# States of two batches summed on TensorE, keys of the first batch made ahead of x, a threshold by a sign on ScalarE, and an order of its own for each engine

## The reference

```python
def step(state, xs):                      # L0: 16 states per channel, 256 channels
    d_t, B_t, C_t, u_t = xs
    dA = jnp.exp(d_t[..., None] * A)
    state = state * dA + (d_t * u_t)[..., None] * B_t[:, None, :]
    return (state, jnp.einsum('ben,bn->be', state, C_t))
y = y + D[None, :, None] * u              # y: the sum over the 16 states
y = y * jax.nn.silu(z)                    # z = layernorm(x)
...
q = rmsnorm(x_n @ Wq, gq)                 # L2: 16 heads of 128
k = rmsnorm(ctx @ Wk, gk)                 # needs the context alone, not x
...
scale = jnp.mean(jnp.abs(w)) + EPS        # L1 ffn, L2 ffn: six weights of 256 x 1024
q = jnp.clip(jnp.round(w / scale), -1.0, 1.0) * scale
...
x = x + tanh(g_xattn[0]) * L0_ssm(ctx, ln(x));  x = x + tanh(g_ffn[0]) * L0_moe(ln(x))
x = x + tanh(g_xattn[1]) * L1_smoothquant(ln(x), fside, ctx);  x = x + tanh(g_ffn[1]) * L1_ternary(ln(x))
x = x + tanh(g_xattn[2]) * L2_attention(ln(x), ctx);  x = x + tanh(g_ffn[2]) * L2_bitlinear(ln(x))
x = x + tanh(g_xattn[3]) * L3_attention(ln(x), ctx);  x = x + tanh(g_ffn[3]) * L3_ternary(ln(x))
```

## Time and profile before

| | us |
|---|---|
| median of 3 runs | 1147.06 |
| lowest, highest | 1143.35, 1147.12 |
| the profiled execution | 1148.34 |
| its span | 1146.6 |
| busy: PE, DVE, ACT, POOL | 837.9, 760.7, 523.6, 322.3 |
| mean granted clock of PE | 0.852 |

### The profile page before, as it was taken

The page is one execution under the profiler, slowest core; times in us unless marked ns, Lnnn a source line. Parts: engine busy times, 40 slices in busy tenths (PEclk is TensorE's granted clock), DMA queues, the critical chain, the costliest instruction groups (busy, mean ns, idle before and its releaser), DMA issues.

```text
span 1146.6 us, 12868 instructions
## 1 busy us (share of the span) xinstructions
PE 837.9 (73%) x3924; PEld 624.4 (54%) x3924; DVE 760.7 (66%) x1812; ACT 523.6 (46%) x1244; POOL 322.3 (28%) x394
## 2 busy tenths in 40 slices
PE   3111676646998977589799885898998769899455
PEld 2000355325666855357578664576886646667234
DVE  5898789874366787955688989554558654355542
ACT  5544543213554544455554553465344435556223
POOL 1433054403132103513444115224110331500204
PEclk9555589759999999789799998898999879989657
DMA  6511524424222202212323104124320221400002
GB/s 219 184 55 51 188 96 147 157 68 146 69 98 97 69 19 69 69 49 90 120 79 108 54 28 120 42 83 142 100 68 28 74 83 42 133 25 23 1 0 65
DMA packets 45476, 96.24 MB, mean 84 GB/s; under 512 B 4824, under 2 KB 16480, under 8 KB 44256
## 3 DMA queue, kind: packets, MB, share of 16 engines
q1 hardware_dynamic: 36192, 70.26, 19.0%
q0 software_dynamic: 9216, 25.17, 7.6%
HBM read 85.97 MB, written 9.44 MB: 83 GB/s over the span
## 4 chain that ended last, share of the span: by engine, by line
PE 45%; DVE 31%; issue 10%; ACT 9%; POOL 5%; DVEq 0%; POOLq 0%; ACTq 0%
PE bk L994 33%; PE bk L1045 7%; DVE ssm_u L1557 6%; DVE ssm_u L1563 2%; DVE ssm_u L1551 2%; PE bk L1240 2%; PE bk L1038 1%; DVE mx L1775 1%; DVE lnbuf L1465 1%; DVE t1A L1586 1%; DVE arB L1788 1%; PE bk L1376 1%; ACT arB L885 1%; DVE t2A L1589 1%; DVE t1B L1871 1%
## 5 line engine op out<-in xcount | busy, mean ns | idle before, releaser
L585 POOL TENSOR_TENSOR sy<-sy,ssm_u 128x512 f32<-128x512 f32 x64 | 86.6, 1354 | 110.6 <-DVE ssm_u L1563 104.2
L994 PE MATMUL bk<-hTA,ringT 128*128 128x256 f32 x448 | 116.6, 407 | 1.1 <-ACT hTB L769 0.7
L994 PE MATMUL bk<-bc,sel 96*128 96x512 bf16 x64 | 29.4, 463 | 97.3 <-DVE ssm_u L1563 93.6
L994 PEld LDWEIGHTS bk<-hTA,ringT 128*128 128x128 f32 x448 | 90.6, 207 | 17.5 <-issue 2.0
L557 POOL TENSOR_TENSOR lnbuf<-lnbuf,mhalf 128x2 f32<-128x2 f32 x32 | 23.4, 730 | 263.9 <-DVE lnbuf L1471 263.9
L1557 DVE TENSOR_TENSOR_SCAN ssm_u<-ssm_da,ssm_u 128x512 f32<-128x512 f32 x64 | 91.1, 1424 | 4.3 <-DVE ssm_u L1551 0.5
L994 PE MATMUL bk<-qk 128*128 128x256 f32 x288 | 80.4, 404 | 6.0 <-ACT arB L885 3.2
L885 ACT ACTIVATE arB<-bk,nb,rqs 128x256 f32<-128x256 f32 x128 | 71.0, 562 | 27.6 <-DVE nb L1778 27.4
L994 PE MATMUL bk<-arB,cx 128*128 128x256 f32 x256 | 69.5, 394 | 11.8 <-DVE qk L1823 8.9
L600 POOL TENSOR_TENSOR arA<-t2A,arA 128x256 f32<-128x256 f32 x44 | 38.0, 865 | 130.2 <-DVE t2A L1589 113.9
L803 ACT ACTIVATE ssm_da<-sdl,nega 128x255 f32<-128x255 f32 x128 | 57.1, 499 | 34.0 <-DVE ssm_u L1557 30.8
(11 more groups left out here) (326 smaller groups left out, 2249.4 us busy)
## 6 DMA issues: line engine op xcount, KB each, us to landing
ringT<-in_w SPq DMA_DIRECT2D x56, 384.0 KB, 3.0
ring<-q3s POOLq DMA_DIRECT2D x32, 384.0 KB, 3.3
ringQ<-in_wqk SPq DMA_DIRECT2D x32, 384.0 KB, 2.9
ring<-q7s POOLq DMA_DIRECT2D x32, 384.0 KB, 3.3
ringM<-m4s SPq DMA_DIRECT2D x32, 256.0 KB, 2.6
q3s<-qk SPq DMA_DIRECT2D x4, 512.0 KB, 7.7
q7s<-qk SPq DMA_DIRECT2D x4, 512.0 KB, 4.3
qk<-in_wo SPq DMA_DIRECT2D x4, 512.0 KB, 4.6
```

The costliest lines, as they stand in the source:

```text
L585: g.tensor_tensor(sy[:, :, :], sy[:, :, :], two(ssm_u[:, n % 3, :]), ALU.add).then_inc(*sig("s0.pool", "y", n))
L994: return t_.matmul(dst, lhsT, rhs, start=start, stop=stop)
```

## The change

1. **States on PE for batches 0 and 1.** `YB = {0: W1, 1: PT}` names a bank for each. In these batches POOL adds nothing; PE adds sy and then the product of each state into the bank, by fp32 products with the identity, 128x512: 17 per batch, 34 in all. The gate multiply reads the bank. Batches 2 and 3 stay on POOL.
2. **Keys of batch 0 ahead.** A new part `keys0` makes the 16 keys of batch 0 and adds their squares into the right half of the norm bank AR, in the banks SC and OP, once `value_output` is done. s4(0) then makes the queries only: its squares and its norm products are 256 wide, and no key is copied. The query and key weights are read eight slots (384 KB each) more often.
3. **Lower threshold by a sign.** ACT computes Sign(w + t), 128x2048, six times; DVE takes the minimum of (w > t) and the sign. The six marks on DVE and one of the two threshold instructions are gone.
4. **Banks and loads.** The group means of `group_ternary` and the products of `value_output` use the two banks SC and OP (four and two before). `weights2`, the refills and copies of the preparation have places of their own; x and the context of batch 1 are loaded first of all; the first reduction of `weights2` stands in the prologue.
5. **Order.** `PLAN` has one table for each engine, chosen by `now[0]`, with more points.

The core of the diff follows; its pieces stand in the order of the file: tables, SP, POOL, ACT, PE, DVE.

```diff
-        wthr, e0 = cut(lnbuf, e0, 2, 6)
+        wthr, e0 = cut(lnbuf, e0, 6)
...
-        GMB, M4B = [SC, PT, OP, SC], [SC, PT]
+        YB = {0: W1, 1: PT}
+        GMB, M4B, KB = [SC, OP], [SC, OP], [SC, OP]
...
+        now = [None]
         PLAN = {
...
-            "state": [((-1.2, 24.56), (2.23, 42.06), (5.66,...
...
+            "pe": {
...
+                "state": {0: ((-1.2, 155.15), (-0.2, 204.66...
...
-            knots = PLAN[part][b]
+            knots = PLAN[now[0]][part][b]
...
+            def fillK():
+                for j in range(NH // 2):
+                    yield at_kp(max(j - 1, 0) - 4)
+                    if j >= NQ:
+                        sp.wait_ge(*at(None, "k0.pe", "k", j - NQ))
+                    sp.dma_start(slotQ(j), a["wqk"][j]).then_inc(dma_sem(f"ringQ{j % NQ}"), 16)
...
+                if b in YB:
+                    return
                 for n in range(NST):
...
+                    yield at_ternary(n + 0.5)
+                    act.wait_ge(*at(None, "prep.dve", "thr", n))
+                    s.activation(q7b[n % 2], stage_slot[n % 2], ACT.Sign, bias=wthr[:, n:n + 1]).then_inc(*sig(K, "sgn3", n))
...
+            def keys0():
+                for j in range(NH // 2):
+                    yield at_kp(j + 0.4)
+                    act.wait_ge(*at(None, "k0.pe", "k", j))
...
+                    s.activation(N4[0][0][:, j % 2, :], KB[j % 2][:, :], ACT.Square).then_inc(*sig("k0.act", "sq", j))
+                    s.activation(kT[:, 2 * j:2 * j + 2, :], halves(KB[j % 2]), ACT.Copy, scale=gqk[:, 2:3]).then_inc(*sig("k0.act", "kT", j))
...
+            def keys0():
+                for j in range(NH // 2 + 1):
+                    if j < NH // 2:
+                        yield at_kp(j)
...
+                        for h in range(2):
+                            i = mm(half(KB[j % 2], h), slotQ(j)[:, (3 * h + 2) * P:(3 * h + 3) * P], cxTs[0][:, :])
...
+                            i = t_.matmul(B4[0][5][0:96, S:], hot[:, 15 - n:111 - n], N4[0][0][:, (j - 1) % 2, h * S:h * S + S],
+                                          start=n == 0, stop=n == NH - 1, skip_group_check=True)
...
+                def add_y(n):
+                    if n == 0:
+                        pe.wait_ge(*at(b, "s0.pool", "yd", 1))
+                        mm(YB[b][:, :], ident[:, :], sy[:, :, :].rearrange("p e t -> p (e t)"), stop=False)
+                    pe.wait_ge(*at(b, "s0.dve", "hc", n))
+                    mm(YB[b][:, :], ident[:, :], ssm_u[:, n % 3, :], start=False, stop=n == NST - 1).then_inc(*sig("sy.pe", "y", n))
...
+                if b == 0:
+                    pe.wait_ge(*at(None, "k0.act", "kT", NH // 2 - 1))
+                    pe.wait_ge(*at(1, "sx.dve", "yg"))
                 transpose_h(b, "s4", h, bank)
...
-                        mm(ring[n % 2][:, S:], w[:, 2 * P:], cxTs[b % 3][:, :]).then_inc(*sig("s4.pe", "kq", n))
+                        if b:
+                            i = mm(ring[n % 2][:, S:], w[:, 2 * P:], cxTs[b % 3][:, :])
...
-                    v.tensor_scalar(wthr[:, 1, n:n + 1], wmean[:, n:n + 1], -0.5, None, ALU.mult).then_inc(*sig(K, "thr", n))
-                    v.tensor_scalar(q7b[n % 2], stage_slot[n % 2], wthr[:, 1, n:n + 1], None, ALU.is_lt).then_inc(*sig(K, "lt", n))
-                                           in1=q7b[n % 2], op0=ALU.is_gt, op1=ALU.subtract).then_inc(*sig(K, "used", n))
+                    dve.wait_ge(*at(None, "prep.act", "sgn3", n))
+                                           in1=q7b[n % 2], op0=ALU.is_gt, op1=ALU.min).then_inc(*sig(K, "used", n))
```

241 lines of the change are left out of this document (157 added, 84 removed), and 210 rows, old and new, of the table PLAN.

## The result

| | before | after |
|---|---|---|
| median of the runs | 1145.55 us (1143.35 to 1147.12) | 1080.59 us (1077.70 to 1082.69, 4 runs) |
| ratio, 95% interval | | 0.942 [0.9393, 0.9447] |
| profiled execution: own time, span | 1148.3, 1146.6 us | 1082.7, 1080.9 us |

The change makes the kernel 65 us faster (the kernel before ran once more beside it, so its median is of four here). Most executions of the kernel before lie near 1144 or near 1149 us, and the profiled one is of the second kind, so a difference of 3 to 5 us between two single traces can be one between executions.

The account below looks back on a forecast made before the run. No one engine bounds the whole: DVE bounds the states, short dependent chains some stretches, PE from 281 to 1001. Terms -8 - 3 + 3 + 2 - 14 - 12 = -32 gave 1116.3, about 1115 by median; range 1086 to 1142.

Parts of the forecast that it names:

- The start: 0 to 110 us: marks gone, faster scans, less reductions of `weights2` and a wait for Sign; -8, between -12 and +3.
- The price of a state: States of batch 0: about 2.6 us of DVE each, with PE's 1.7 plus a spreading of 0.61 hidden under it.
- 110 to 281: Three terms: 110 to 156 closer order -3; 156 to 231 batch 1 states +3; 231 to 281 keys among short steps +2.
- The rival that PE gives the 28.6 us back: 110 to 281: idle time can't take identity products and keys, so the stretch grows by all of it; 1139, chance 0.17.
- The rival of the clock: Added products raise PE's clock to 0.97 in the two chain-bound stretches, -10; with more from order 1097; chance 0.18.
- the main case: Whole kernel: the summed forecast of -32, 1115 us, own range 1103 to 1129, chance 0.48.
- The contention of POOL: Batch 1 scans: POOL's expert additions might keep slowing them, so perhaps 1 of 2.1 us is had; sum 1 us worse.
- 281 to 392: PE-bound stretch: batch 0's keys leave it, 13.8 us of PE with nothing hiding them; -14, or -8 if other limits.
- 392 to 1001: PE bound with 105 us of holes; no work removed, the new order gains -12, bounds -30 and +12.
- the table of waits: 392 to 1001: PE waits of 19.9 us at spreadings and 16.1 at POOL's split; a third of these 36 us gained.
- The rival "order costs more": Attention 1 starts later, 33 us on the path, decided beyond some 20 us; +13, 1160, chance 0.10.
- The last stretch: From the first head of batch 3 on: same PE queue, change 0, 140 to 146 us as before.

Follow-up runs that it names:

- experiment 7: Changed kernel with selector copies, third sign and its combination moved behind the first scans: 1077.26, again 1076.62 us beside the changed kernel's 1080.84; copies alone: 1078.93.
- experiment 4: Changed kernel with one work change undone at a time: states of batches 0 and 1 on POOL 1087.96 us; keys in s4(0) 1097.69; mark on DVE 1087.22.
- experiment 5: Kernel before with single instructions moved: PE's spreadings of batch 2 states 13 and 14 later, 1145.11 us; DVE's multiplications of states 12 and 13 earlier, 1144.76.
- experiments 3 and 1: Both on the changed kernel's code. 3: old order and old work, leaving moved waits, banks, loads, places, 1134.41 us. 1: new order with old work, 1109.45 us.
- experiment 6: Kernel before, s5 to s7 and heads of batches 1 to 3 later by 12 or 26: 1184.63, 1176.76 us. Changed kernel, five chunks back among heads: 1100.08.

## Why the prediction was wrong

**The start, -8 forecast, -8.3 measured**, is right in sum and wrong in its parts. From first scan to last product it went from 68.9 to 54.2 us, -14.7, where I had -9.3 from scans and marks; and the first scan came 6.4 later, where I had +2 for reductions and a wait. Part of both is one shift: a sign and a combination that stood in the loop stand ahead of it now (experiment 7). I had checked the wait for the sign in the loop and not in the prologue, where nothing stands between it and the combination. The price of a state (2.6 against 2.65), its cover on PE and the identity product held. What I had not seen is that ACT's table for the exponential is loaded behind the third sign.

**110 to 281, +2 forecast, -0.2 measured.** The sum holds, the place doesn't. The first query comes 8.5 us earlier (280.8 against 289.3), near the 7 that I had named. I had the keys from 231 to 281; they stand at 195 to 226 between the last chunks, so the stretch up to the end of batch 1's loop got 10.9 us longer and the one behind it 11.1 shorter (8.6 in the changed kernel run again). The rival that PE gives the 28.6 us back failed: PE was busy 67.67 of 73.2 us there at 0.98, so the time was there. The rival of the clock came true in part. The pair of windows in experiment 4 shows that the keys lift it right behind them; over the stretch to the first query it is 0.81 in place of 0.69 in one execution of the changed kernel and hardly more than before in the other:

```profile
228.20:283.30 55.10, 33.38 (x160) 26.05 (x160) 29.86 (x103) 12.84 (x32) 13.25 (x21) 0.72 0.27 77
```

I had set the rising clock against the main case, and both happened.

**The contention of POOL** was my doubt of 1 us: the additions for the experts might go on slowing the scans of batch 1. They didn't (19.58 us for 16), and yet the rule that raised the doubt holds. The Trainium skill (GPSIMD Engine Reference, section Specifications) has GpSimd and VectorE share their SBUF interfaces and contend where a VectorE instruction has two SBUF inputs; the trace agrees, with 1.62 beside an addition that began first, and none beside L1860. I had asked which addition slows a scan. Both do; without POOL's states the other just comes early enough to miss it.

**281 to 392, -14 forecast, -19.4 measured, -17.1 by experiment 4.** The mechanism was right: nothing hid the keys in s4(0), and PE's busy time in the stretch fell by 14.6, from 131.0 to 116.4. The rest is idle time, 15.2 before and 10.4 after. Against the other trace of the same instructions (143.0 us, experiment 5) the stretch fell by 16.2, so about 3 of the 19.4 are the execution's.

**392 to 1001, -12 forecast, -40.7 measured.** This is the step that failed: the term of -12 for the order, which came out at more than three times its size. I took the order's worth from the table of waits: 36 us named in two rows, a third of them had, and -30 for nearly all. Experiment 5 shows for its two largest waits that they have no such meaning: to take them away moved next to nothing. And the gain isn't bounded by the table: from before to after PE's idle time in the middle fell by 28.6 us, of which 17.4 stand in the two rows, and its busy time by 12.1, for nearly the same records (2358, 2372) at clock 0.95 in place of 0.92; 469.6 times 0.92/0.95 is 454.8. Neither the 69 us of idle time outside the two rows nor the clock in the middle was in my sum. The row that spoke for both was in the earlier trace rows: 105 us of holes at clock 0.92, right behind 111 us at 0.97.

What the order does there is shown in part. With the work undone it takes the middle from 555.4 to 521.6 us (experiments 3 and 1), 33.8 less, of which 25 are left over the whole kernel. Nine chunks left attention 2, which is 23.3 us shorter, and the stretch that took them in didn't grow, with six s3 chunks gone from it. Moving such chunks without aligning the other steps loses: 28 to 36 us by a common shift, and 19 for five chunks put back, of which their place explains some 4 (both experiment 6). The moved waits, banks and places of experiment 3 give 10.0 of the 40.7. How the rest divides between chunks and alignment stays open: the tables of the engines fit only together, so an engine's new order wasn't tried beside the old order of the others.

**The rival "order costs more", 1160**, was passed at its own point and failed in its price. Attention 1 starts 234.6 us behind the start of attention 0, before 209.4: 25 us later, where I had it decide from 20. But attention 0 starts 45.7 us earlier (318.5 against 364.2), since the same chunks and spreadings no longer stand ahead of it; I had put them on the path behind it and not taken them off ahead. The two common shifts of experiment 6 were slower, as the rival feared, at 1177 and 1185.

**The last stretch, 140 to 146 us forecast, 148.6 measured**, with the same queue: PE's busy time is 102.80 against 99.17, and the clock 0.74 against 0.77. A last queue that is the same once more, in the kernel of experiment 7, took 144.8 us:

```profile
926.20:1071.00 144.80, 97.98 (x468) 71.81 (x467) 67.96 (x199) 55.11 (x156) 23.53 (x35) 0.78 0.09 27
```

So the 3 us are of the size by which two executions of one queue differ, and no run parts them from the change.

**The range** was too narrow at the bottom because the order and the clock stood as rivals, 1115 or 1097, where the case that came had both: with the order at its bound of -30 and the clock's -10 my own terms make 1087, still short of 1081.

## What to carry to other kernels

Don't size a new order by the rows of its wait table. In this kernel a wait at the head of one of several coupled queues was handed to the next owner when it was removed. Look at the idle time and the clock of a stretch as a ceiling instead, and ask which independent work could be put there: here the expert chunks of the next batch, ahead of an attention in which PE was full. Move such work on every engine that has a part in it, and move what depends on it too; five chunks moved without their followers cost some 15 us more than my estimate for their place. Where work is to be moved ahead, price it with its loads and its places: the three changes of work gave nothing in the old order, with the keys at places that I guessed, and 29 us in the new one. And compare two single traces of one kernel before reading a difference of 3 us in a stretch.

## What the runs showed of the hardware

- A scan on DVE and an addition on POOL that meet don't both slow down: in the state loops of batches 0 and 1 the one that began first kept its time (addition 0.73, scan 1.22) and the other was drawn out (scan 1.62, addition 1.57). Which one paid was set by the order in which they started.
- Six passes of ACT over 128x2048 with a bias read per partition (Sign) took 1998 ns each; passes of that size without one, three of Sign among them, took 1893 to 1899.
- PE's busy time in the middle was 469.6 us at clock 0.92 and 457.5 at 0.95, for nearly the same records. The seven traces with the order of before or a common shift of it have 0.91 to 0.93 there; the changed kernel, run again, has 0.95. So the order that filled holes got busy time back as well. In the last stretch the clock was between 0.74 and 0.78 for one and the same queue (148.6 and 144.8 us): there it is a matter of the execution.
